# Conv and attention chain on one core: the MLP's first block ahead of the attention's last gate and residual

## The chip, the cores and the metric

The kernel runs on one core of one Trainium2 chip. The metric is the device time of one execution in microseconds; the time given is the median of three runs. The core has TensorE (matrix products, rows marked PE, and PEld for the loading of its weights), VectorE (DVE), ScalarE (ACT), GpSimd (POOL) and the sync engine (SP), each with its own list of instructions that it works off in order. What ties them together are semaphores: `wait_ge` holds an engine, and everything behind it in its list, until a count is reached, and `then_inc` raises a count when an instruction is done.

## What is computed

Four layers are applied to x of shape (4, 128, 96, 96): a mag/phase 1x1 convolution (layer 0), a selective-scan block (layer 1), a linear-attention block with an MLP (layer 2), and a 3x3 convolution with binary weights and activations (layer 3). The change lies in layer 2, between attention and MLP:

```python
ti = silu(img2tok(_dwconv(tok2img(ti), dwc_w, dwc_b)))
ta = _attn(ti, ...)                       # linear attention plus the lepe depthwise 3x3
t = shortcut + ta * act_res @ outproj_w + outproj_b
t = t + img2tok(_dwconv(tok2img(t), cpe2_w, cpe2_b))
tn2 = _ln(t, n2_g, n2_b)                  # over the 128 channels
mlp = gelu(tn2 @ fc1_w + fc1_b) @ fc2_w + fc2_b
t = t + mlp
```

## The kernel before

An image has its 128 channels on the partitions and its 96x96 pixels along them. It is cut into NB = 12 blocks of 8 rows, 768 columns. The four images are worked off one after the other, and within one image the stages follow each other. Each engine's list is made by `pipelined` or `overlapped` (L53 and L71): in round t a stage with lag l works on block t - l, and within a round the stages stand in the order in which the list names them. `overlapped` does that for several runs with a start round each. This written order is the only scheduling there is: what stands later in a list can't overtake. All counts carry a head start of 3 blocks, so waits for block b - 2 cost nothing for the first blocks.

The attention's second half, per block: TensorE computes queries, denominator, numerator and the lepe convolution; VectorE adds the lepe taps (`add_taps`, L1573, signal `f2_lepe`); GpSimd multiplies with the gate (`ta`, L711, signal `f2_ta`); TensorE projects (`project`); VectorE adds the result to the image in region 1 (`residual2`, L1590, two halves, signal `f2_t2`). GpSimd also makes the rotated queries (`turned`, L705 and L706). On GpSimd `ta` has lag 3 and `turned` lag 1; on VectorE `residual2` has lag 3 and `add_taps` lag 2.

The MLP's stage per block b:

- the cpe2 convolution of nine taps. ScalarE makes tap 0 and two terms (`first_tap` L841, `term` L862, the second of which waits for `g_t` of block b - 2), GpSimd adds the two terms (`add_term`, L678), VectorE adds taps 3 to 6 (`chain_tap`, L220), tap 7 (L1602) and tap 8 (L1607, signal `g_t`). The tiles of this chain are two per step, used in turn, and lie in region 0 over the attention's image.
- the norm. TensorE subtracts the mean with a product (`g_centre`, signal `g_yc`), ScalarE squares (`g_squares`, L957), TensorE averages (`g_variance`, into bank 6, which the projection used too), ScalarE does Ln and Exp (`g_root`, L962 and L964, with a table load ahead), VectorE multiplies (`g_normalise`, L1613, signal `g_tn`).
- the MLP. TensorE's four `up` and four `down` products, ScalarE's four Gelu (L969), VectorE's residual `x3` (L1617), ScalarE's `sign` (L974) for layer 3.

`g_centre` of block b waits for `g_tn` of block b - 1, and `up(0)` of block b for `g_tn` of block b. One round of TensorE holds ten products: four up, four down, a variance and a centre.

Before the change VectorE's list holds the whole attention and then the MLP; GpSimd's holds `ta` and `turned` of all blocks and then the additions; ScalarE waits, ahead of its MLP list, for `f2_lepe` and `f2_ta` of all twelve blocks. In round 3 of the MLP ScalarE does block 3's tap, its two terms and then block 0's root; VectorE in its round 3 does block 2's six taps and then block 0's normalise.

After the MLP's twelfth block, the next image's layer 0 (L1373 on VectorE first) follows, while layer 3 of the present one runs on TensorE (L1068).

Of the kernel before, what the change touches and what calls it, by code (L numbers as in the profile page):

```python
# [52 lines left out]
def pipelined(eng, count, stages):  # L53

    deepest = max(lag for lag, _ in stages)
    for t in range(count + deepest):
        for lag, stage in stages:
            if 0 <= t - lag < count:
                stage(t - lag, (t - lag) % 2)
# [11 lines left out]
def overlapped(eng, count, runs):  # L71

    stop = max(start + max(lag for lag, _ in stages) for start, stages in runs) + count
    for t in range(stop):
        for start, stages in runs:
            for lag, stage in stages:
                if 0 <= t - start - lag < count:
                    stage(t - start - lag, (t - start - lag) % 2)


def build(nc, t, out):

    B, _, S, _ = t["x"].shape
    NB = S // ROWS
# [12 lines left out]
    def done(i, b):  # L97

        return i * NB + (b + (1 + CREDIT))

    def steps(i, b, each, step):

        return i * (NB * each) + (b * each + step)
# [6 lines left out]
    with ctx:  # L110
# [8 lines left out]
        def pair(bank):  # L119

            return psum[:, bank:bank + 2, 0:HC]
# [9 lines left out]
        def padded(k):  # L131
            return R[k][:, 0:SP * SP].rearrange("p (h w) -> p h w", w=SP)

        def flat(k, b):
            return R[k][:, ds(BLK * b, BLK)]

        def prow(k, b, dh=0, dw=0, rows=ROWS, skip=0):

            return padded(k)[:, ds(ROWS * b + (1 + dh + skip), rows), 1 + dw:1 + dw + S]
# [3 lines left out]
        def tile(n):  # L143
            return work[:, n * BLK:(n + 1) * BLK]

        def region_tile(k, n):
            return R[k][:, n * BLK:(n + 1) * BLK]

        def halves(ap):
            return ap.rearrange("p (a c) -> p a c", a=2)  # L150
# [58 lines left out]
        def col(name, n=0, rows=slice(0, P)):  # L209
            return cols[rows, at[name] + n:at[name] + n + 1]  # L210

        def tap_weight(conv, tap):
            return col("taps", 9 * convs.index(conv) + tap_column(tap))
# [17 lines left out]
        def signal(name, owner):  # L231
            s = sem(name)
            block_signals.append((s, owner))
            return s
# [68 lines left out]
        f2_qs = signal("f2_qs", "g")  # L303
# [7 lines left out]
        f2_lepe = signal("f2_lepe", "v")  # L311
        f2_ta = signal("f2_ta", "g")
        f2_out = signal("f2_out", "p")
        f2_t2 = signal("f2_t2", "v")
# [42 lines left out]
        def all_done(eng, i, *signals):  # L357

            eng.wait_ge(ready, 1)
            for s in signals:  # L360
                k = 4 if s is g_fc1 or s is g_gelu else 1
                eng.wait_ge(s, i * (NB * k) + (NB + CREDIT) * k)
# [59 lines left out]
        def by_row(ap):  # L422
            return ap.rearrange("p (r w) -> p r w", w=S)

        def is_first(b):
            return isinstance(b, int) and b == 0
# [195 lines left out]
        def _(g):  # L622
            credit(g, "g")
            g.wait_ge(ready, 1)
            def middle(i):
# [48 lines left out]
                def add_term(conv, n):  # L674
                    def stage(b, p):
                        g.wait_ge(term_done[n], termed(i, b))
                        g.wait_ge(tap_done[n - 1], tapped(i, b))
                        g.tensor_tensor(chain_tile(conv, n, p), chain_tile(conv, n - 1, p), chain_tile(conv, n, p),  # L678
                                        ALU.add).then_inc(tap_done[n], 1)
                    return stage  # L680
# [29 lines left out]
                    g.wait_ge(f2_lepe, done(i, b))  # L710
                    g.tensor_tensor(tile(2 + p), tile(2 + p), flat(2, b), ALU.mult).then_inc(f2_ta, 1)  # L711

                pipelined(g, NB, [(3, ta), (1, turned)])

                taps = [add_term("cpe2", tap) for tap in TERM_TAPS]
                pipelined(g, NB, [(0, tap) for tap in taps])

                all_done(g, i, g_t)
                clear_frame(signs())
# [6 lines left out]
        def _(a):  # L726
# [61 lines left out]
            def middle(i, following_runs):  # L788
# [177 lines left out]
                def gelu(j):  # L966
                    def stage(b, p):
                        a.wait_ge(g_fc1, steps(i, b, 4, 4 * CREDIT + j + 1))
                        a.activation(halves(tile(4 + j)), pair(0), ACT.Gelu, bias=col("fc1_o", j)).then_inc(g_gelu, 1)  # L969
                    return stage  # L970

                def sign(b, p):
# [1 line left out]
                    a.activation(signs()[:, ds(ROWS * b + 1, ROWS), 1:1 + S],  # L974
                                 flat(3, b).rearrange("p (r w) -> p r w", w=S), ACT.Sign).then_inc(g_sign, 1)

                all_done(a, i, f2_lepe, f2_ta)
                tap, first, second = terms("cpe2", 1, 0, f2_t2, g_t)
                mlp = [(4, gelu(0)), tap, (6, sign), (4, gelu(1)), first, second, (4, gelu(2)), (3, g_root),
                       (4, gelu(3)), (2, g_squares)]  # L980
                overlapped(a, NB, [(0, mlp)] + following_runs)

# [9 lines left out]
        def _(pe):  # L992
# [7 lines left out]
            for k in range(4):  # L1000
                pe.matmul(psum[:, 1, P * (k // 2):P * (k // 2) + P], xp_r[:, P * k:P * (k + 1)], dt_r[:, P * k:P * (k + 1)],
                          start=(k % 2 == 0), stop=(k % 2 == 1))
# [24 lines left out]
            def static(ap):  # L1027
                return lambda s: ap[:, HC * s:HC * (s + 1)]
# [56 lines left out]
            def middle(i, following_runs):  # L1085
# [111 lines left out]
                turned = region_tile(3, 9)  # L1197
# [4 lines left out]
                for n in range(NT):  # L1202
                    last = pe.matmul(psum[:, 6, 300:301], region_tile(3, 10)[:, P * n:P * (n + 1)], col("one"),
                                     start=(n == 0), stop=(n == NT - 1))
# [45 lines left out]

                def g_variance(b, p):
                    pe.wait_ge(g_sq, done(i, b))
                    pe.wait_ge(g_log, done(i, b - 1))
                    product(6, [(avg128, static(tile(2 + p)))]).then_inc(g_var, 1)

# [8 lines left out]
                def down(j):  # L1264
                    def stage(b, p):
# [11 lines left out]
                mlp = [(4, up(0)), (5, down(3)), (4, up(1)), (4, down(0)), (4, up(2)), (4, down(1)),  # L1277
                       (3, g_variance), (4, up(3)), (4, down(2)), (2, g_centre)]
# [10 lines left out]
        def _(v):  # L1289
# [133 lines left out]
            def middle(i, following_runs):  # L1423
# [80 lines left out]
                left = side_tap("cpe1", 0, 0, 1, e1["centre"])  # L1504
                right = side_tap("cpe1", 0, 0, 2, e1["centre"])
# [14 lines left out]
                left = side_tap("dwc", 3, 0, 1, e2_centre)  # L1520
                right = side_tap("dwc", 3, 0, 2, e2_centre)
# [71 lines left out]

                left = side_tap("lepe", 0, 4, 1, f2_centre)
                right = side_tap("lepe", 0, 4, 2, f2_centre)
                pipelined(v, NB, [(2, left), (2, right), (0, query_phi), (1, weigh), (3, residual2), (2, add_taps)])


                def tap_7(b, p):
                    acc = by_row(chain_tile("cpe2", 2, p))  # L1600
# [3 lines left out]

                def tap_8(b, p):
                    v.wait_ge(g_tap7, done(i, b))
                    v.scalar_tensor_tensor(out=by_row(flat(3, b)), in0=prow(1, b, *TAPS[8]),  # L1607
                                           scalar=tap_weight("cpe2", TAPS[8]), in1=by_row(chain_tile("cpe2", 2, p)),
                                           op0=ALU.mult, op1=ALU.add).then_inc(g_t, 1)

                def g_normalise(b, p):
                    v.wait_ge(g_rstd, done(i, b))
                    v.tensor_tensor(halves(flat(2, b)), halves(tile(2 + p)), pair(2), ALU.mult).then_inc(g_tn, 1)  # L1613

                def x3(b, p):
# [2 lines left out]
                                           in1=halves(flat(3, b)), op0=ALU.add, op1=ALU.add).then_inc(g_x3, 1)  # L1618

                taps = [chain_tap(v, i, "cpe2", tap, 1, lambda p: chain_tile("cpe2", 2, p)) for tap in VECTOR_TAPS]  # L1620
                mlp = [(1, taps[0]), (1, taps[1]), (5, x3), (1, taps[2]), (1, taps[3]), (1, tap_7), (1, tap_8),
                       (3, g_normalise)]
                overlapped(v, NB, [(0, mlp)] + following_runs)

            overlapped(v, NB, [(0, begin(0, False)), (NB, conv_run(0))])
            for i in range(B - 1):
# [89 lines left out]
```

## Time and profile before

| | |
|---|---|
| median of 3 runs | 3650.93 us (3647.74 to 3663.47) |
| the profiled execution | 3652.96 us, span 3651.0 us |
| busy: TensorE, VectorE, ScalarE, GpSimd | 2936.3, 2437.7, 2368.8, 1101.4 us |
| TensorE's clock granted, mean of the span | 0.937 |
| data moved by DMA | 274.91 MB, mean 75 GB/s |

The row of 40 slices shows the four images as four repeats of the same pattern: TensorE at 9 tenths through most of the MLP, lower in the selective scan. A busy TensorE is not one at its peak, since the ends of pipelined products are modelled. In the timelines a row merges instructions of one line that follow each other; "x4" says how many.

### The profile page before, as it was taken

How to read it: one execution, taken by the hardware profiler on the slowest of the kernel's cores; microseconds unless marked ns; L12 is line 12 of the kernel's file. 1: busy time of each engine (PE TensorE's matmuls, PEld its weight loads, DVE VectorE, ACT ScalarE, POOL GpSimd, SP SyncE). 2: the span in 40 equal slices, each digit the busy share in tenths (PEclk: the TensorE clock that was granted, in tenths of full speed). 3: DMA queues.
4: the chain of work that ended last, by engine and by line, in shares of the span. 5: the costliest groups of instructions: out<-in, count | busy, mean ns of one | idle time of the engine just before them, and what ended most of it. 6: DMA issues, size and time to landing. Idle time of an engine off the chain costs nothing. (4 is left out here: it accounts for less than half of the span.)

```text
span 3651.0 us, 45449 instructions
## 1 busy us (share of the span) xinstructions
PE 2936.3 (80%) x17500; PEld 1593.8 (44%) x17500; DVE 2437.7 (67%) x2565; ACT 2368.8 (65%) x2681; POOL 1101.4 (30%) x612
## 2 busy tenths in 40 slices
PE   3688876969969877778996888776998788769699
PEld 2344335435534434434553433443555344354355
DVE  5787657865579657676466964768636886576761
ACT  2888545468689745437778864644868977454484
POOL 0236103642025500463103530146310453025430
PEclk9999998989999999899998999988999999989899
DMA  2001473500200157440020034643002005564101
GB/s 67 18 1 40 121 199 118 161 9 1 73 23 1 53 141 208 118 119 9 0 91 5 1 93 123 200 132 91 9 9 87 0 0 142 139 182 135 41 1 52
DMA packets 137227, 274.91 MB, mean 75 GB/s; under 512 B 17139, under 2 KB 93622, under 8 KB 137014
## 3 DMA queue, kind: packets, MB, share of 16 engines
q1 hardware_dynamic: 137014, 272.01, 26.7%
q8 instruction: 141, 2.31, 0.3%
q14 instruction: 72, 0.59, 0.1%
HBM read 194.07 MB, written 77.88 MB: 74 GB/s over the span
## 5 line engine op out<-in xcount | busy, mean ns | idle before, releaser
L1499 DVE SCALAR_TENSOR_TENSOR work<-region,cols,work 128x768 f32<-128x768 f32 x288 | 373.3, 1296 | 8.4 <-ACT work L902 3.3
L678 POOL TENSOR_TENSOR region<-region 128x768 f32<-128x768 f32 x96 | 225.4, 2352 | 350.6 <-ACT region L862 344.6
L1017 PE MATMUL psum<-region,m_fc 128*128 128x384 f32 x768 | 282.6, 491 | 11.8 <-ACT work L969 11.8
L1017 PE MATMUL psum<-region,m_cen 128*128 128x384 f32 x384 | 159.7, 541 | 158.8 <-DVE region L1613 60.9
L1270 PE MATMUL psum<-work,m_fc 128*128 128x384 f32 x768 | 282.3, 491 | 0.0
L654 POOL TENSOR_TENSOR work<-work,region 128x768 f32<-128x768 f32 x96 | 174.5, 1818 | 211.5 <-DVE work L1429 211.5
L642 POOL TENSOR_TENSOR work<-work 128x768 f32<-128x768 f32 x48 | 102.1, 2130 | 442.6 <-ACT work L783 416.1
L220 DVE SCALAR_TENSOR_TENSOR region<-region,cols 128x768 f32<-128x768 f32 x192 | 223.9, 1166 | 12.3 <-POOL region L678 8.3
L969 ACT ACTIVATE work<-psum,cols 128x768 f32<-128x768 f32 x192 | 173.1, 901 | 87.6 <-PE psum L1017 82.9
L1017 PE MATMUL psum<-work,m_avg 128*128 128x384 f32 x576 | 216.9, 500 | 16.0 <-ACT work L824 8.0
L1416 DVE SCALAR_TENSOR_TENSOR work<-region,cols,work 128x768 f32<-128x768 f32 x144 | 195.7, 1379 | 40.9 <-POOL work L642 37.5
L1017 PEld LDWEIGHTS psum<-region,m_fc 128*128 128x128 f32 x768 | 143.4, 191 | 122.8 <-ACT work L969 35.3
L693 POOL COPY region<-work 128x768 f32<-128x768 f32 x4 | 3.3, 827 | 632.9 <-DVE work L1536 632.9
L933 ACT ACTIVATE region<-psum,cols 128x768 f32<-128x768 f32 x48 | 43.2, 901 | 232.5 <-PE psum L1017 232.5
L1270 PEld LDWEIGHTS psum<-work,m_fc 128*128 128x128 f32 x768 | 142.1, 190 | 109.5 <-DVE region L1617 19.2
L1017 PEld LDWEIGHTS psum<-region,m_cen 128*128 128x128 f32 x384 | 69.4, 201 | 250.0 <-issue 117.2
L1017 PE MATMUL psum<-region,m_w_dt 128*128 128x384 f32 x384 | 147.1, 509 | 21.9 <-DVE work L1429 11.6
L1444 DVE TENSOR_TENSOR_SCAN work<-work,psum 128x768 f32<-128x768 f32 x88 | 159.6, 1814 | 3.1
L1017 PEld LDWEIGHTS psum<-work,m_avg 128*128 128x128 f32 x576 | 107.8, 193 | 108.2 <-ACT work L824 29.7
L1617 DVE SCALAR_TENSOR_TENSOR region<-psum,cols,region 128x768 f32<-128x768 f32 x48 | 48.9, 1018 | 157.5 <-PE psum L1270 157.5
L705 POOL TENSOR_TENSOR region<-work,region 128x768 f32<-128x768 f32 x48 | 90.8, 1892 | 207.8 <-DVE work L1584 207.8
L670 POOL TENSOR_TENSOR region<-work,region 64x768 f32<-64x768 f32 x48 | 115.5, 2406 | 121.0 <-DVE work L1468 121.0
(234 smaller groups left out, 7530.5 us busy)
## 6 DMA issues: line engine op xcount, KB each, us to landing
work<-scratch_cpe SPq DMA_DIRECT2D x192, 196.0 KB, 4.1
work<-scratch_dwc SPq DMA_DIRECT2D x192, 196.0 KB, 4.2
work<-scratch_lepe SPq DMA_DIRECT2D x192, 196.0 KB, 4.1
region<-in_tab_ch SPq DMA_DIRECT2D x48, 768.0 KB, 5.9
region<-in_x SPq DMA_DIRECT2D x48, 384.0 KB, 3.5
region<-in_tab_tok SPq DMA_DIRECT2D x48, 384.0 KB, 3.2
out<-work SPq DMA_DIRECT2D x48, 384.0 KB, 2.5
scratch_cpe<-region SPq DMA_DIRECT2D x44, 392.0 KB, 4.7
```

The source lines that it names most:

```text
L220: eng.scalar_tensor_tensor(out=tgt, in0=prow(k, b, *TAPS[n]), scalar=tap_weight(conv, TAPS[n]), in1=tgt, op0=ALU.mult, op1=ALU.add).then_i ...
L642: g.tensor_tensor(tile(4 + p), tile(p), tile(2 + p), ALU.add).then_inc(b_taps[0], 1)
L654: g.tensor_tensor(tile(2 + p), tile(p), flat(2, sweep_block(sweep, b)), ALU.mult).then_inc(c["du"], 1)
L670: g.tensor_tensor(flat(1, b)[0:CM], tile(2 + p)[CM:P], flat(1, b)[CM:P], ALU.mult).then_inc(d_gate, 1)
L678: g.tensor_tensor(chain_tile(conv, n, p), chain_tile(conv, n - 1, p), chain_tile(conv, n, p), ALU.add).then_inc(tap_done[n], 1)
L705: g.tensor_tensor(region_tile(3, 4 + p), tile(p), region_tile(3, 2 * p), ALU.mult).then_inc(f2_qc, 1)
L969: a.activation(halves(tile(4 + j)), pair(0), ACT.Gelu, bias=col("fc1_o", j)).then_inc(g_gelu, 1)
L1017: last = pe.matmul(psum[:, bank + s, 0:HC], weights[:, :], moving(s), start=(n == 0), stop=(n == len(terms) - 1))
L1270: last = pe.matmul(psum[:, 4 + s, 0:HC], fc2[:, P * j:P * (j + 1)], static(tile(4 + j))(s), start=(j == 0), stop=(j == 3))
L1416: v.scalar_tensor_tensor(out=by_row(tile(6 + p)) if n == 4 else sofar, in0=prow(3, b, *scan_tap(n)), scalar=col("l1taps", n), in1=sofar, o ...
L1444: v.tensor_tensor_scan(way(tile(6 + p)), way(tile(4 + p)), way(bu_flat), initial=start, op0=ALU.mult, op1=ALU.add).then_inc(c["h"], 1)
L1499: v.scalar_tensor_tensor(out=by_row(tile(acc + p)), in0=prow(k, b, *TAPS[n]), scalar=tap_weight(conv, TAPS[n]), in1=by_row(tile(acc + p)), ...
```

## The change

ScalarE's wait for all of `f2_lepe` and `f2_ta` becomes a wait for `f2_lepe` of block 6, after which the attention no longer reads the rows of region 0 on which the chain tiles lie. GpSimd's two additions of block 0 stand between `ta(10)` and `ta(11)`, those of block 1 behind `ta(11)`. On VectorE the MLP's run begins in round NB + 1 and stands ahead of the attention within a round, so block 0's six tap operations stand between `add_taps(11)` and `residual2(11)`. `g_root` of block 0 stands first in ScalarE's round 3, and `g_normalise` of block 0 first in VectorE's round 3; for all other blocks both keep their places. Two waits are added for the first block: tap 8, which writes to region 3, waits for the last `f2_qs`, since region 3 holds `turned`'s tables and results; `g_variance` waits for the last `f2_t2`, since `residual2` reads bank 6.

```diff
--- before.py
+++ after.py
@@ -710,10 +710,8 @@
                     g.wait_ge(f2_lepe, done(i, b))
                     g.tensor_tensor(tile(2 + p), tile(2 + p), flat(2, b), ALU.mult).then_inc(f2_ta, 1)
 
-                pipelined(g, NB, [(3, ta), (1, turned)])
-
                 taps = [add_term("cpe2", tap) for tap in TERM_TAPS]
-                pipelined(g, NB, [(0, tap) for tap in taps])
+                overlapped(g, NB, [(0, [(3, ta), (1, turned)]), (NB + 1, [(0, tap) for tap in taps])])
 
                 all_done(g, i, g_t)
                 clear_frame(signs())
@@ -974,9 +972,11 @@
                     a.activation(signs()[:, ds(ROWS * b + 1, ROWS), 1:1 + S],
                                  flat(3, b).rearrange("p (r w) -> p r w", w=S), ACT.Sign).then_inc(g_sign, 1)
 
-                all_done(a, i, f2_lepe, f2_ta)
                 tap, first, second = terms("cpe2", 1, 0, f2_t2, g_t)
-                mlp = [(4, gelu(0)), tap, (6, sign), (4, gelu(1)), first, second, (4, gelu(2)), (3, g_root),
+                root_first = (3, lambda b, p: g_root(b, p) if is_first(b) else None)
+                root_later = (3, lambda b, p: None if is_first(b) else g_root(b, p))
+                a.wait_ge(f2_lepe, done(i, NB // 2))
+                mlp = [root_first, (4, gelu(0)), tap, (6, sign), (4, gelu(1)), first, second, (4, gelu(2)), root_later,
                        (4, gelu(3)), (2, g_squares)]
                 overlapped(a, NB, [(0, mlp)] + following_runs)
 
@@ -1250,6 +1250,8 @@
 
                 def g_variance(b, p):
                     pe.wait_ge(g_sq, done(i, b))
+                    if is_first(b):
+                        pe.wait_ge(f2_t2, done(i, NB - 1))
                     pe.wait_ge(g_log, done(i, b - 1))
                     product(6, [(avg128, static(tile(2 + p)))]).then_inc(g_var, 1)
 
@@ -1593,8 +1595,7 @@
 
                 left = side_tap("lepe", 0, 4, 1, f2_centre)
                 right = side_tap("lepe", 0, 4, 2, f2_centre)
-                pipelined(v, NB, [(2, left), (2, right), (0, query_phi), (1, weigh), (3, residual2), (2, add_taps)])
-
+                attention = [(2, left), (2, right), (0, query_phi), (1, weigh), (3, residual2), (2, add_taps)]
 
                 def tap_7(b, p):
                     acc = by_row(chain_tile("cpe2", 2, p))
@@ -1604,6 +1605,8 @@
 
                 def tap_8(b, p):
                     v.wait_ge(g_tap7, done(i, b))
+                    if is_first(b):
+                        v.wait_ge(f2_qs, done(i, NB - 1))
                     v.scalar_tensor_tensor(out=by_row(flat(3, b)), in0=prow(1, b, *TAPS[8]),
                                            scalar=tap_weight("cpe2", TAPS[8]), in1=by_row(chain_tile("cpe2", 2, p)),
                                            op0=ALU.mult, op1=ALU.add).then_inc(g_t, 1)
@@ -1618,9 +1621,11 @@
                                            in1=halves(flat(3, b)), op0=ALU.add, op1=ALU.add).then_inc(g_x3, 1)
 
                 taps = [chain_tap(v, i, "cpe2", tap, 1, lambda p: chain_tile("cpe2", 2, p)) for tap in VECTOR_TAPS]
-                mlp = [(1, taps[0]), (1, taps[1]), (5, x3), (1, taps[2]), (1, taps[3]), (1, tap_7), (1, tap_8),
-                       (3, g_normalise)]
-                overlapped(v, NB, [(0, mlp)] + following_runs)
+                norm_first = (3, lambda b, p: g_normalise(b, p) if is_first(b) else None)
+                norm_later = (3, lambda b, p: None if is_first(b) else g_normalise(b, p))
+                mlp = [norm_first, (1, taps[0]), (1, taps[1]), (5, x3), (1, taps[2]), (1, taps[3]), (1, tap_7), (1, tap_8),
+                       norm_later]
+                overlapped(v, NB, [(NB + 1, mlp), (0, attention)] + [(NB + 1 + start, run) for start, run in following_runs])
 
             overlapped(v, NB, [(0, begin(0, False)), (NB, conv_run(0))])
             for i in range(B - 1):
```

## Rows read from the trace of the kernel before

**Rows 1.** The page, part 1: busy time of each engine.
```profile
PE 2936.3 (80%) x17500; PEld 1593.8 (44%) x17500; DVE 2437.7 (67%) x2565; ACT 2368.8 (65%) x2681; POOL 1101.4 (30%) x612
```

**Rows 2.** Table by stage: stretch, us, busy time of each engine, granted clock, DMA.
```profile
1629.00:1659.00 30.00, 5.85 (x8) 2.35 (x8) 27.74 (x21) 11.22 (x13) 16.69 (x8) 0.61 0.00 0
...
1680.00:1760.00 80.00, 77.80 (x236) 43.28 (x235) 55.68 (x48) 69.85 (x77) 29.85 (x12) 1.00 0.02 5
```

**Rows 3.** Chain that ended last, MLP of the last image: start, us, what.
```profile
3488.75 2.82 PE psum L1017 x8
3491.57 1.29 PE psum L1270 x4
...
3502.34 2.82 PE psum L1017 x8
```

**Rows 4.** Timeline of VectorE, second image: start, us, what, [idle before, releaser].
```profile
1622.78 0.95 DVE L1573 TENSOR_TENSOR work<-work,psum 128x768 f32<-128x768 f32 x1 [1.08 <-issue]
...
1628.64 1.14 DVE L1590 SCALAR_TENSOR_TENSOR region<-psum,cols,region 128x384 f32<-128x384 f32 x2 [4.90 <-PE psum L1017]
...
1631.51 8.55 DVE L220 SCALAR_TENSOR_TENSOR region<-region,cols 128x768 f32<-128x768 f32 x4 [1.73 <-POOL region L678]
...
1641.15 1.02 DVE L1607 SCALAR_TENSOR_TENSOR region<-region,cols 128x768 f32<-128x768 f32 x1
...
1648.77 2.44 DVE L1607 SCALAR_TENSOR_TENSOR region<-region,cols 128x768 f32<-128x768 f32 x1
...
1651.13 5.59 DVE L220 SCALAR_TENSOR_TENSOR region<-region,cols 128x768 f32<-128x768 f32 x4
...
1658.75 0.95 DVE L1613 TENSOR_TENSOR region<-work,psum 128x768 f32<-128x768 f32 x1
...
1659.61 4.17 DVE L220 SCALAR_TENSOR_TENSOR region<-region,cols 128x768 f32<-128x768 f32 x4
...
1674.42 0.95 DVE L1613 TENSOR_TENSOR region<-work,psum 128x768 f32<-128x768 f32 x1 [8.52 <-ACT work L964]
```

**Rows 5.** Timeline of ScalarE, the same turn.
```profile
1625.78 1.03 ACT L841 ACTIVATE region<-region,cols 128x768 f32<-128x768 f32 x1 [14.66 <-issue]
...
1645.19 0.81 ACT L957 ACTIVATE work<-psum 128x768 f32<-128x768 f32 x1 [2.05 <-PE psum L1017]
...
1653.49 0.90 ACT L962 ACTIVATE work<-psum,cols 128x768 f32<-128x768 f32 x1
...
1654.42 0.84 ACT L964 ACTIVATE work<-work 128x768 f32<-128x768 f32 x1
```

**Rows 6.** Timeline of GpSimd, the same turn.
```profile
1616.26 2.53 POOL L711 TENSOR_TENSOR work<-work,region 128x768 f32<-128x768 f32 x1
...
1623.82 1.80 POOL L711 TENSOR_TENSOR work<-work,region 128x768 f32<-128x768 f32 x1 [5.02 <-DVE work L1573]
...
1627.71 10.48 POOL L678 TENSOR_TENSOR region<-region 128x768 f32<-128x768 f32 x5 [2.09 <-ACT region L862]
```

**Rows 7.** Timeline of TensorE, the same turn.
```profile
1642.22 2.93 PE L1017 MATMUL psum<-region,m_cen 128*128 128x384 f32 x4 [13.63 <-DVE region L1607]
...
1659.84 2.90 PE L1017 MATMUL psum<-region,m_cen 128*128 128x384 f32 x4 [10.86 <-DVE region L1613]
1662.53 1.35 PE L1017 MATMUL psum<-region,m_fc 128*128 128x384 f32 x3
```

**Rows 8.** Timeline of VectorE, last image.
```profile
3408.37 0.96 DVE L1573 TENSOR_TENSOR work<-work,psum 128x768 f32<-128x768 f32 x1 [1.08 <-issue]
...
3460.46 0.95 DVE L1613 TENSOR_TENSOR region<-work,psum 128x768 f32<-128x768 f32 x1 [8.96 <-ACT work L964]
```

**Rows 9.** Table by stage, after the second image's turn.
```profile
1662.90:1676.00 13.10, 11.09 (x34) 5.95 (x33) 4.51 (x5) 11.85 (x13) 3.62 (x2) 1.00 0.08 16
```

**Rows 10.** Timeline of VectorE, from the first image's MLP into the next.
```profile
932.16 1.02 DVE L1617 SCALAR_TENSOR_TENSOR region<-psum,cols,region 128x768 f32<-128x768 f32 x1 [8.10 <-PE psum L1270]
933.09 0.55 DVE L1373 TENSOR_TENSOR region<-region 128x384 f32<-128x384 f32 x1
```

## The prediction

> **What bounds the kernel now.** The totals come first: TensorE is busy for 80% of the span, VectorE 67%, ScalarE 65%, GpSimd 30% [rows 1]. No engine is full, so the question is which wait stands last in which stage. The table by stage answers it for the place that is edited. In the MLP's steady rounds TensorE is busy 77.8 of 80 us; in the 30 us between attention and MLP of the second image it is busy 5.9 us, while VectorE is busy 27.7 [rows 2]. So TensorE sets the pace after the turn, and VectorE inside it. The chain that ended last confirms the steady part: one block enters TensorE every 13.59 us (3502.34 less 3488.75) [rows 3], and each round closes over `g_normalise`, so when the second block is normalised fixes when all later blocks are.
>
> VectorE's own sequence over the turn is then read row by row [rows 4]. `add_taps(11)` (L1573) starts at 1622.78 and ends at 1623.73. VectorE idles 4.90 us until the last projection is there, does `residual2(11)` (L1590), idles 1.73 for GpSimd, does block 0's four chain taps, tap 7 and tap 8 until 1642.17, block 1's until 1651.2, block 2's until 1658.8, and only then block 0's normalise (L1613) at 1658.75. It does block 3's taps, idles 8.52, and normalises block 1 at 1674.42. ScalarE had finished block 0's root at 1655.26 (1654.42 + 0.84) [rows 5]. ScalarE itself stood idle 14.66 us before its first cpe2 tap [rows 5], at the wait for `f2_ta`. I count each turn from the start of `add_taps(11)` to the start of the second `g_normalise`: 51.64 us here, 52.09 in the last image [rows 4, 8]; the other two images read 51.94 and 51.65.
>
> **The change, part by part** (times of the second image).
>
> (a) ScalarE no longer waits for `f2_ta`. It is free at about 1611.1, 14.66 before 1625.78 [rows 5]. Blocks 0 and 1 take three operations of about 1 us each, so both are done by 1617; the third block's wait for GpSimd's sums. Nothing in the attention stands behind them on ScalarE, so their price is zero.
>
> (b) GpSimd adds block 0's two terms between `ta(10)`, which ends at 1618.79 (1616.26 + 2.53), and `ta(11)`, which can't start before 1623.82. Two additions cost 2.10 each in the run of five (10.48 / 5) [rows 6], so they end at 1623.0 and fit in GpSimd's idle 5.02. Price zero if that cover holds; each 1 us of overrun would delay `ta(11)`, but not VectorE, which now has block 0's taps first.
>
> (c) VectorE's round: block 0's six taps stand before `residual2(11)`. They start at 1623.8 instead of 1631.51. A tap costs 1.05 alone (4.17 / 4), and 2.44 against 1.02 (the rows of L1607) when it meets a GpSimd addition, so 1.42 more for each addition met [rows 4]. Before, block 0 met three (8.55 - 4.17 = 3.1 x 1.42), block 1 two (2.44 in its last tap, 1.4 in its first four, which are shown for block 2), block 2 one (5.59 for four taps where 4.17 would do), block 3 none. Now GpSimd has `ta(11)`, block 1's two sums and the first of block 2 in block 0's stretch: four. Block 0 takes 6 x 1.05 + 4 x 1.42 = 12.0 and ends at 1635.8, 6.4 earlier. `residual2(11)` has been moved behind six taps; its two halves take 1.14 [rows 4], with a gap to 1637.1. Who waits for it: the new wait in `g_variance(0)`, and ScalarE's taps of blocks 10 and 11, more than 100 us later. Block 1 meets one sum: 6.3 + 1.4, to 1644.8.
>
> (d) The root first. TensorE's centre product starts at 1635.8; ScalarE's squares began 2.97 after it (1645.19 against 1642.22) and take 0.81; the variance product takes the same 2.97 at the low clock; Ln and Exp 0.93 + 0.84 [rows 5, 7]. That is 1635.8 + 2.97 + 0.85 + 2.97 + 1.8 = 1644.4. The table load stands in the variance's shadow. The added wait in `g_variance(0)` for `f2_t2(11)` ends at 1637.1, before the squares end at 1639.7: zero. ScalarE's block 3 taps are queued behind the root, about 3 us for nobody on the path.
>
> (e) The normalise first. Block 0 is normalised at 1644.8, when root and block 1's taps end within half a microsecond of each other: 13.9 us earlier than 1658.75.
>
> (f) What is late next. The second normalise followed the first by 15.67 us (1674.42 - 1658.75), the length of the path over TensorE and ScalarE, which would put it at 1660.5. But VectorE still owes blocks 2 and 3 before it: 0.95 for the normalise, then twice 6.3, and each block now meets two sums (block 3 met none before, because VectorE was waiting when they came): 0.95 + 2 x (6.3 + 2.84) = 19.2. The second normalise starts at 1664.0. So of 13.9 us, 3.5 are given back, and 10.4 stay. The same by idle time: 4.90 + 1.73 + 8.52 = 15.15 of VectorE's idle go, three additions more are met (9 for 6), 4.3, and 10.9 remain; the two agree within my roundings.
>
> (g) From there each round is the old one, earlier: in a steady round VectorE has idle time, TensorE none. The last block's residual hands over to the next image's first operation (L1373) in the same microsecond, and nothing else was waited for [rows 10], so an image's gain passes to the next. By image the counted turn becomes 41.3 us: gains of 10.7, 10.4, 10.4 and 10.8, **42.3 us** in sum. No DMA moves against another; SP's queue is not edited, its next loads of x shift with the MLP. Against the profiled execution (3652.96, span 3651.0) that gives 3610.7, and against the median of 3650.93, from which it stands 2 us off, **3608.6**.
>
> The uncertain price is the meeting of VectorE and GpSimd. The rows show 0 below (an addition that meets nobody) and 1.42 for each one met; nothing shows a gain. GpSimd's additions take 1.8 alone, so 1.8 is the upper end. With no additions met in block 3, the time goes to the next bound, 1660.5 or so: 13.9 an image. With 1.8 for each of nine: 3.4 less, 7.0 an image. I take 1.42, which six meetings before show without exception.
>
> By the Trainium skill ("SBUF — State Buffer", SBUF: two separate sides) the pair of ports that VectorE and GpSimd share is an exclusive lock, for two-input VectorE instructions against GpSimd reads, held for a whole instruction, so a tap can wait for a full addition. The trace agrees in kind (2.44 for 1.02). By the rule the worst sum is the 7.0 an image just worked out, by the rows 10.4.
>
> **The rivals.**
> Less contention: VectorE is not the bound at the second normalise, and the round trip of 15.67 us is. For it: ScalarE's operations could shift so that block 4's sums come after block 3's taps. Against it: my block 4 sums start at 1655.2, as block 3's taps do. 13.9 an image, 55.8 in sum: **3595**.
> More contention: seven an image, 28 in sum: **3623**. Against it: in block 0 of before, five additions in a run cost three taps 1.4 each, no more.
> Absorbed: the gain is real at the turn but a later stage of the first three images waits for something unmoved (a DMA, GpSimd's clearing). Then the last image alone counts, 10.8: **3640**. Against it: [rows 10].
> It doesn't do what it says: block 0's taps stay late, since some wait in ScalarE's or GpSimd's new order holds (the third block's first term waits for block 0's first sum). Then nothing moves: **3651**. I find no such wait for block 0.
> Slower, by TensorE's clock: the 30 us of the turn have a mean grant of 0.61 [rows 2]; its products run at 1.2 GHz and then take 2.69 (1662.53 less 1659.84) for 1.29 at 2.4 GHz [rows 3, 7]. The new order makes a second idle of about 3 us before the second normalise. If the clock stayed low over the next rounds, each round of ten products would cost 14.0 more; it decides from 0.74 of a round an image (10.4 / 14.0), and two rounds give 4 x (28 - 10.4) = 70 more: **3721**. Against it: with 10.86 us of idle before, the clock was granted in full from 1662.9, 3 us after work began again at 1659.84 [rows 7, 9].
>
> **How the numbers follow.** Forecast 0.60; less contention 0.13; more contention 0.11; absorbed 0.07; nothing 0.06; slower 0.03. The range takes the first three (0.84), with 3 to 5 us of uncertainty of the runs (before read 3647.7 to 3663.5): 3590 to 3632. One half per cent, about what a measurement can tell, is 18.3 us: faster means below 3632.7. Faster is 0.60 + 0.13 + 0.11 and 0.02 of the partly absorbed: 0.86; same 0.11; slower 0.03.
>
> **What the profile after would show.** (a) ScalarE's first cpe2 tap about 12 us before VectorE's last `add_taps`; (b) `ta(11)` at 1.0 us after `add_taps(11)` starts, as now; (c) taps directly behind it, no idle, and the residual after 13.1 us; (d, e) the first normalise 22 us after `add_taps(11)` starts, for 35.97; (f) the second after 41.3, for 51.64, with no VectorE idle between, and a pause of TensorE before it; (g) pitch 13.59 unchanged. Wrong it would be if VectorE idles before the first normalise (the root is late), if the second stays at more than 48 (contention), or if TensorE's low clock reaches beyond the second normalise.

## The result, and the profile after

The changed kernel takes 3617.82 us (median, 3604.73 to 3620.03), the kernel before 3650.68 beside it (3647.74 to 3663.47). The ratio is 0.990, with a 95% interval of 0.9883 to 0.9917: 33 us, 0.9%, faster. Forecast were 42 us. The profiled execution took 3617.15, its span is 3615.3, 35.7 less than 3651.0.

VectorE in the second image's turn after the change; it answers to [rows 4]. VectorE's line numbers are one to three higher than before: L1575 is `add_taps`, L1592 `residual2`, L1603 and L1610 taps 7 and 8, L1616 `g_normalise`, L1620 `x3`; L220 is still taps 3 to 6. On ScalarE they are two lower, so L962, which was the root's Ln, is now its Exp; L1272 on TensorE is `down`.

```profile
1614.03 0.95 DVE L1575 TENSOR_TENSOR work<-work,psum 128x768 f32<-128x768 f32 x1 [1.08 <-issue]
1614.90 8.44 DVE L220 SCALAR_TENSOR_TENSOR region<-region,cols 128x768 f32<-128x768 f32 x4
1623.37 2.44 DVE L1603 SCALAR_TENSOR_TENSOR region<-region,cols 128x768 f32<-128x768 f32 x1
1625.85 1.02 DVE L1610 SCALAR_TENSOR_TENSOR region<-region,cols 128x768 f32<-128x768 f32 x1
1626.78 1.14 DVE L1592 SCALAR_TENSOR_TENSOR region<-psum,cols,region 128x384 f32<-128x384 f32 x2
1627.84 5.59 DVE L220 SCALAR_TENSOR_TENSOR region<-region,cols 128x768 f32<-128x768 f32 x4
...
1635.45 0.95 DVE L1616 TENSOR_TENSOR region<-work,psum 128x768 f32<-128x768 f32 x1
1636.31 6.83 DVE L220 SCALAR_TENSOR_TENSOR region<-region,cols 128x768 f32<-128x768 f32 x4
...
1645.17 7.03 DVE L220 SCALAR_TENSOR_TENSOR region<-region,cols 128x768 f32<-128x768 f32 x4
...
1654.23 0.95 DVE L1616 TENSOR_TENSOR region<-work,psum 128x768 f32<-128x768 f32 x1
...
1662.10 1.02 DVE L1620 SCALAR_TENSOR_TENSOR region<-psum,cols,region 128x768 f32<-128x768 f32 x1 [4.95 <-PE psum L1272]
...
1670.45 0.95 DVE L1616 TENSOR_TENSOR region<-work,psum 128x768 f32<-128x768 f32 x1 [1.81 <-ACT work L962]
```

The three idles of [rows 4] (4.90, 1.73, 8.52) are gone: from 1614.03 to the second normalise VectorE never waits. Counted from the start of the last `add_taps`, the first three normalises of the second image come at 21.42, 40.20 and 56.42, where they came at 35.97, 51.64 and 65.23. The second is 11.4 earlier, the third only 8.8, and 8.8 it stays to the twelfth (178.8 for 187.6). What took the difference stands in TensorE's timeline of the same rounds:

```profile
1650.21 1.45 PE L1272 MATMUL psum<-work,m_fc 128*128 128x384 f32 x4
1655.32 2.90 PE L1017 MATMUL psum<-region,m_cen 128*128 128x384 f32 x4 [3.66 <-DVE region L1616]
1658.01 2.76 PE L1017 MATMUL psum<-region,m_fc 128*128 128x384 f32 x4
1660.57 1.49 PE L1272 MATMUL psum<-work,m_fc 128*128 128x384 f32 x4
...
1671.55 1.53 PE L1017 MATMUL psum<-region,m_cen 128*128 128x384 f32 x4 [0.37 <-DVE region L1616]
```

TensorE waits 3.66 us for the second normalise, and its next two products take 2.90 and 2.76 where one takes 1.53 and 1.45 at 2.4 GHz. The table by stage of the same stretch (us, busy of TensorE, weight loads, VectorE, ScalarE, GpSimd, granted clock, DMA) says why:

```profile
1653.80:1660.70 6.90, 5.38 (x9) 2.98 (x10) 3.32 (x4) 0.81 (x1) 0.00 (x0) 0.51 0.00 0
1660.70:1670.45 9.75, 9.75 (x32) 5.56 (x31) 6.43 (x6) 8.30 (x10) 4.97 (x2) 1.00 0.00 0
```

The clock was granted at 0.51 from 1653.8, still inside the pause, until 1660.7. The third normalise is 16.22 behind the second, 2.63 more than the steady 13.59 (16.43 in the last image, the same 16.2 in the others).

The sum closes. Over the four images the stretch from the last `add_taps` to the third normalise is 261.7 us before and 226.0 after: 35.7, as much as the spans differ. That it fits to a tenth is luck: the stretches between the twelfth normalise and the next image's last `add_taps` vary by 10 us among the images of before alone (704.9, 710.4 and 700.0), and only their sums agree (2115.3 before, 2115.4 after).

### The profile page after: what moved, and what is told of

Read it like the earlier page. It is cut to its first block, busy times and chain, and to the rows that moved or that the text cites. A ratio compares the mean times of both kernels' runs of the same rounds, so it can differ in the third digit from the quotient of the medians.

```text
span 3615.3 us, 45449 instructions
## 1 busy us (share of the span) xinstructions
PE 2944.2 (81%) x17500; PEld 1596.7 (44%) x17500; DVE 2452.4 (68%) x2565; ACT 2367.4 (65%) x2681; POOL 1106.2 (31%) x612
## 3 DMA queue, kind: packets, MB, share of 16 engines
q1 hardware_dynamic: 137014, 272.01, 26.9%
## 4 chain that ended last, share of the span: by engine, by line
PE 48%; DVE 27%; issue 10%; ACT 8%; DMA 4%; POOL 1%; SPq 1%; DVEq 0%; POOLq 0%; ACTq 0%
PE psum L1017 30%; PE psum L1272 5%; PE psum L1037 5%; DVE work L1418 5%; DVE work L1446 5%; PE psum L1068 3%; DVE region L220 3%; DVE region L1547 3%; DVE psum L1437 2%; DVE work L1431 2%; PE psum L1228 2%; PE psum L1229 2%; DMA work<-scratch_dwc 2%; DVE region L1491 1%; DMA region<-in_tab_tok 1%
## 5 line engine op out<-in xcount | busy, mean ns | idle before, releaser
L1272 PE MATMUL psum<-work,m_fc 128*128 128x384 f32 x768 | 282.8, 492 | 0.0
L220 DVE SCALAR_TENSOR_TENSOR region<-region,cols 128x768 f32<-128x768 f32 x192 | 239.8, 1249 | 4.0
L1272 PEld LDWEIGHTS psum<-work,m_fc 128*128 128x128 f32 x768 | 143.1, 191 | 110.8 <-DVE region L1620 19.2
L1017 PE MATMUL psum<-region,m_w_dt 128*128 128x384 f32 x384 | 147.3, 510 | 21.5 <-DVE work L1431 11.1
L1620 DVE SCALAR_TENSOR_TENSOR region<-psum,cols,region 128x768 f32<-128x768 f32 x48 | 48.9, 1018 | 168.4 <-PE psum L1272 168.4
L1037 PE MATMUL psum<-work,m_dwc_shifted 64*32 64x384 f32 x2304 | 116.5, 537 | 45.9 <-DMA work<-scratch_dwc 45.9
```

The source lines that it names most:

```text
L220: eng.scalar_tensor_tensor(out=tgt, in0=prow(k, b, *TAPS[n]), scalar=tap_weight(conv, TAPS[n]), in1=tgt, op0=ALU.mult, op1=ALU.add).then_i ...
L1017: last = pe.matmul(psum[:, bank + s, 0:HC], weights[:, :], moving(s), start=(n == 0), stop=(n == len(terms) - 1))
L1037: last = pe.matmul(psum[32 * j:32 * j + 32, bank + s, 0:HC], shifted[conv][half, c0:c0 + 32], rows[half, j, :, dw:dw + S], start=(fresh an ...
L1272: last = pe.matmul(psum[:, 4 + s, 0:HC], fc2[:, P * j:P * (j + 1)], static(tile(4 + j))(s), start=(j == 0), stop=(j == 3))
```

## The experiments

Each is an edit of the changed kernel. Turns are counted from the start of the last `add_taps`; where the images agree, one number stands for all four. "Turns" in a sum means the four stretches from there to the third normalise: 261.7 us before, 226.0 in the changed kernel. In the diffs "..." stands for lines left out.

**The pause filled.** TensorE works through its pause.

```diff
+                def fill(block, count):
+                    def stage(b, p):
+                        if isinstance(b, int) and b == block:
+                            pe.wait_ge(g_log, done(i, b - 1))
+                            for n in range(count):
+                                pe.matmul(psum[:, 6, 384:512], avg128[:, :], ident[:, :], start=True, stop=True)
+                    return stage
...
-                       (3, g_variance), (4, up(3)), (4, down(2)), (2, g_centre)]
+                       (3, g_variance), (4, up(3)), (4, down(2)), (2, fill(2, 15)), (2, g_centre)]
```

> The changed kernel, plus 15 small products (128 columns, to unused columns of bank 6) on TensorE just ahead of block 2's centre product, where TensorE pauses 3.66 us in each image before the second normalise. The products change no result. Turn times are counted from the start of the last add_taps; changed kernel: first normalise 21.42, second 40.20, third 56.43 (16.23 after the second, where a steady round is 13.59). Theory (the pause drops TensorE's clock, and the low clock lengthens the next round by 2.65): the second normalise stays at 40.2 to 40.5, the clock is not lowered after it, the third follows at 13.6 to 13.9, and four images give 9 to 11 us, a span near 3605. Rival (that round is long because VectorE or ScalarE have work left over from the turn): the second to third distance stays at 16.2 and the time at 3617.

Measured: 3604.0 us (3603.34 to 3606.23), ratio to before 0.9877 (0.9862 to 0.9892), span 3601.7. The second normalise stays at 40.2 (40.5 in the last image), the third comes 13.6 behind it, at 53.8 (54.1 in the last). TensorE's timeline, second image; L1284 is the fill, whose 15 products show as 30 rows, and L1624 the normalise:

```profile
1646.65 3.51 PE L1284 MATMUL psum<-m_ident,m_avg 128*128 128x128 f32 x30
1650.46 1.53 PE L1017 MATMUL psum<-region,m_cen 128*128 128x384 f32 x4 [0.30 <-DVE region L1624]
1651.83 1.45 PE L1017 MATMUL psum<-region,m_fc 128*128 128x384 f32 x4
```

The pause is filled for 3.51 us, the centre product waits 0.30 and takes 1.53. With the same second normalise and VectorE's list untouched, 2.6 us an image are back. So the long round was the clock's, and the clock followed the pause; work left over on VectorE or ScalarE is excluded, since it was the same here. The turns are 10.4 us shorter than the changed kernel's; the span is 13.6 shorter, the rest falling elsewhere in the images.

**The second normalise earlier.** If the pause comes from VectorE's list, the list can be mended.

```diff
+                norm_second = (3, lambda b, p: g_normalise(b, p) if b == 1 else None)
-                norm_later = (3, lambda b, p: None if is_first(b) else g_normalise(b, p))
+                norm_later = (3, lambda b, p: None if b < 2 else g_normalise(b, p))
...
-                mlp = [norm_first, (1, taps[0]), (1, taps[1]), (5, x3), (1, taps[2]), (1, taps[3]), (1, tap_7), (1, tap_8),
+                mlp = [norm_first, (1, taps[0]), (1, taps[1]), (5, x3), (1, taps[2]), (1, taps[3]), norm_second, (1, tap_7), (1, tap_8),
```

> The changed kernel, with the second block's normalise between taps 6 and 7 of block 3 on VectorE instead of behind tap 8. Theory (VectorE's list sets the second normalise, whose root is ready at 36.9; the pause sets the clock): the second normalise comes at 37.2 to 37.6 for 40.20, TensorE's pause shrinks from 3.66 to under 1 us, the clock stays high and the third follows at 13.6, at 51 for 56.43: 5.4 an image, 21 us in all, a time near 3596. Rival (the debt of VectorE is only moved: two taps of block 3, six of block 4 and a residual still stand before the third normalise): the third normalise comes at 54 or later, 9 us in all or less, a time of 3608 or more.

Measured: 3592.76 us (3589.5 to 3593.58), ratio to before 0.9846 (0.9829 to 0.9863). The second normalise comes at 38.1 to 38.5, the third at 51.7 to 52.1 in three images and at 53.4 in the first, where a stretch of 3.4 us at the low clock, from 40.2 on, remained. TensorE's wait for it, second image, and VectorE's next rounds:

```profile
1647.61 1.53 PE L1017 MATMUL psum<-region,m_cen 128*128 128x384 f32 x4 [1.29 <-DVE region L1616]
```
```profile
1646.52 0.95 DVE L1616 TENSOR_TENSOR region<-work,psum 128x768 f32<-128x768 f32 x1
...
1651.76 1.02 DVE L1620 SCALAR_TENSOR_TENSOR region<-psum,cols,region 128x768 f32<-128x768 f32 x1 [0.33 <-PE psum L1272]
...
1660.10 0.95 DVE L1616 TENSOR_TENSOR region<-work,psum 128x768 f32<-128x768 f32 x1 [1.81 <-ACT work L962]
```

VectorE's debt (two taps of block 3, a residual, six taps of block 4) fits in the round with 1.81 to spare, so the rival falls. The second normalise is about 0.8 later than I expected, since the four taps ahead of it met GpSimd twice and ended behind the root (7.15 us in the second image, for 4.17; they ended at 38.6, the root at 37.6). This version beats both kernels. Its turns are 16.7 us shorter than the changed kernel's (226.0 - 209.3): 1.7 to 2.1 an image by the earlier normalise, 2.6 to 2.9 in three images and 1.0 in the first by the clock. The median is 25 us lower than the changed kernel's; the 8 us beyond the turns lie in stretches whose lists are the same, so the time came out near the expected 3596 partly by luck.

**The same with a short fill** (six products ahead of the centre product, the fill of above).

> The kernel with the second block's normalise between taps 6 and 7, plus 6 small products on TensorE ahead of block 2's centre product (unused columns of bank 6, no result changed). Without the products one image of four still had a granted clock of 0.50 from 40.2 to 43.6, and its third normalise came 15.3 after the second for 13.6 in the others. Theory (that is the same mechanism, by the pause of 1.3 us and its position): all four images have 13.6 and the low stretch after the second normalise is gone; 0 to 2 us less than without the products, a time of 3588 to 3593, so within the measurement. Rival (six products only delay the centre product): the third normalise comes 1 us later in every image, 4 us more in all.

Measured: 3593.04 us (3588.86 to 3596.12), ratio 0.9868 (0.9849 to 0.9886), not distinguishable from the one without, whose interval overlaps. The kernel before took 3641.89 us beside this run and the two single runs of `fill_turn` and `small_adds` below, where it took 3650.43 beside the others, so times of the two groups can't be compared directly; the turns can. In its profile all four images have 13.6 between second and third normalise, and no low stretch follows the second; the turns sum to 207.2, for 209.3 without the fill. The clock part is as expected; the time lies at the upper edge of what I had given and tells nothing. In one execution each this can't prove that the short fill always helps: three of four images were without a low stretch before it.

**The turn alone**: `g_root` and `g_normalise` of block 0 at their old places.

```diff
-                mlp = [root_first, (4, gelu(0)), tap, (6, sign), (4, gelu(1)), first, second, (4, gelu(2)), root_later,
+                mlp = [(4, gelu(0)), tap, (6, sign), (4, gelu(1)), first, second, (4, gelu(2)), (3, g_root),
...
-                mlp = [norm_first, (1, taps[0]), (1, taps[1]), (5, x3), (1, taps[2]), (1, taps[3]), (1, tap_7), (1, tap_8),
-                       norm_later]
+                mlp = [(1, taps[0]), (1, taps[1]), (5, x3), (1, taps[2]), (1, taps[3]), (1, tap_7), (1, tap_8),
+                       (3, g_normalise)]
```

> The changed kernel with g_root and g_normalise of block 0 at their old places, so only the turn (block 0's taps ahead of the last gate and residual, ScalarE's early start) is left. By my steps: first normalise at about 30.6 (root late behind block 3's terms, normalise behind block 2's taps), second 15.7 later at 46.3, set by the path over TensorE and ScalarE and not by VectorE, third 13.6 later at 59.9: 5.3 an image against before, 21 in all. If the turn alone brought all, the third normalise would come at 56.4.

Measured: normalises at 30.46, 46.1 to 46.5 and 59.7 to 60.1; time 3625.22 in one run. VectorE, second image:

```profile
1647.46 0.94 DVE L1616 TENSOR_TENSOR region<-work,psum 128x768 f32<-128x768 f32 x1
1648.32 4.17 DVE L220 SCALAR_TENSOR_TENSOR region<-region,cols 128x768 f32<-128x768 f32 x4
...
1663.54 0.95 DVE L1616 TENSOR_TENSOR region<-work,psum 128x768 f32<-128x768 f32 x1 [8.93 <-ACT work L962]
```

VectorE again waits 8.93 for the second root: without the early normalise the path over TensorE and ScalarE is the bound, as before. The turn alone is worth 22.0 us over the four images (261.7 - 239.7).

**The order alone**: the lists of before at the turn, with root and norm first.

```diff
-                overlapped(g, NB, [(0, [(3, ta), (1, turned)]), (NB + 1, [(0, tap) for tap in taps])])
+                pipelined(g, NB, [(3, ta), (1, turned)])
+                pipelined(g, NB, [(0, tap) for tap in taps])
...
-                a.wait_ge(f2_lepe, done(i, NB // 2))
+                all_done(a, i, f2_lepe, f2_ta)
...
-                overlapped(v, NB, [(NB + 1, mlp), (0, attention)] + [(NB + 1 + start, run) for start, run in following_runs])
+                pipelined(v, NB, attention)
+                overlapped(v, NB, [(0, mlp)] + following_runs)
```

> The kernel before with g_root and g_normalise of block 0 first in their rounds, without the turn. By my steps: first normalise at 28.4 for 35.97, but VectorE then owes blocks 2 and 3, so the second comes at 47.2 for 51.63 with a pause of TensorE of about 3 us before it, the clock drops, and the third is at 63.4 for 65.23: 1.8 an image, 7 in all. If VectorE's debt did not count, the second would come 15.7 after the first, at 44.1, and the gain would be 7.5 an image, 30 in all.

Measured: 26.9, 46.0 and 61.1 to 61.2 in three images (28.0, 47.1 and 63.5 in the first); 3638.66 us in one run, 14.9 us over the turns (261.7 - 246.8), twice what I expected. VectorE, second image (lines one higher again):

```profile
1647.29 0.95 DVE L1617 TENSOR_TENSOR region<-work,psum 128x768 f32<-128x768 f32 x1
...
1666.40 0.94 DVE L1617 TENSOR_TENSOR region<-work,psum 128x768 f32<-128x768 f32 x1
```

The mechanism is as expected: the second normalise is 19.1 behind the first and VectorE never waits between them. The sizes were off twice. Block 1's taps met one GpSimd addition where I had kept two (block 3's terms stand behind the root now), 1.4 us. And after the pause the clock cost 2.8 us in one image and 1.4 to 1.6 in three, where the low stretch was 3.4 us long for 6.9. (In the first image the first normalise waited 1.03 for its root, behind a variance product of 2.93 at the low clock.) The two halves give 22.0 and 14.9 and together 35.7: nearly additive, 1.2 less.

**TensorE kept busy in the turn**, ahead of the first centre product, where it idles after the last projection.

```diff
+                def warm(block, count):
+                    def stage(b, p):
+                        if isinstance(b, int) and b == block:
+                            pe.wait_ge(f2_phiz, done(i, NB - 1))
+                            for n in range(count):
+                                pe.matmul(psum[:, 2, 384:512], avg128[:, :], ident[:, :], start=True, stop=True)
+                    return stage
...
-                       (3, g_variance), (4, up(3)), (4, down(2)), (2, g_centre)]
+                       (3, g_variance), (4, up(3)), (4, down(2)), (2, warm(0, 24)), (2, g_centre)]
```

> The changed kernel, plus 24 small products (128 columns, to unused columns of bank 2) on TensorE ahead of block 0's centre product, in the idle after the last projection. The products change no result. Theory (before the second normalise VectorE's list is the bound and TensorE's clock costs nothing): centre and variance of block 0 run faster than 2.97 us, the root is ready earlier, but the first normalise stays at 21.42, the second at 40.2 and the third at 56.4. Rival (the low clock at the turn costs time too): the first normalise moves 1 to 2 us earlier, and the second with it.

Measured: first normalise at 21.45 in three images and 23.1 in the last, second at 39.7 (40.6 in the last), third at 56.2 in two images, 54.7 in the first and 55.9 in the last; 3608.26 in one run. TensorE, second image (48 rows are the 24 products):

```profile
1618.18 6.92 PE L1284 MATMUL psum<-m_ident,m_avg 128*128 128x128 f32 x48
1624.93 1.46 PE L1017 MATMUL psum<-region,m_cen 128*128 128x384 f32 x4
```

The centre product takes 1.46 where it took 2.93, and in three images the first normalise doesn't move: the low clock ahead of it costs nothing there, because VectorE's list is the bound. The last image shows what an earlier root can do instead:

```profile
3394.09 2.66 DVE L1618 SCALAR_TENSOR_TENSOR region<-region,cols 128x768 f32<-128x768 f32 x1
```
```profile
3394.14 1.80 POOL L678 TENSOR_TENSOR region<-region 128x768 f32<-128x768 f32 x1 [4.06 <-ACT region L860]
```

The root is ready 1.3 earlier than in the changed kernel (18.7 for 20.1), so ScalarE's terms of block 3 behind it are earlier too, and GpSimd's addition of them begins 1.3 earlier (20.6 for 21.9). In the last image it begins 0.05 us behind the start of block 1's tap 8 (L1618), which takes 2.66 for 1.02; in the others it begins 0.08 to 0.23 behind it, and the tap keeps its 1.02. There block 2's first four taps take 6.29 for 6.83, which is the 0.5 by which the second normalise comes earlier; neither theory had it. The run's time lies 9 us under the changed kernel's median, but its turns account for 2.9 of them (226.0 - 223.1), and the kernel before was itself 8.8 lower beside this run (3641.89 for 3650.68).

**The meetings removed.** GpSimd's additions for blocks 0 to 4 are cut to 64 of 768 columns, so that VectorE has almost nothing to wait for. In the other 704 columns of these blocks a part of the convolution's terms is left out, so this kernel computes something else there.

```diff
+                        cut = slice(0, 64) if isinstance(b, int) and b < 5 else slice(0, BLK)
-                        g.tensor_tensor(chain_tile(conv, n, p), chain_tile(conv, n - 1, p), chain_tile(conv, n, p),
-                                        ALU.add).then_inc(tap_done[n], 1)
+                        g.tensor_tensor(chain_tile(conv, n, p)[:, cut], chain_tile(conv, n - 1, p)[:, cut],
+                                        chain_tile(conv, n, p)[:, cut], ALU.add).then_inc(tap_done[n], 1)
```

> The changed kernel with GpSimd's cpe2 additions cut from 768 to 64 columns for blocks 0 to 4 of each image, so the terms of the other columns are left out of the result there. Only VectorE's meetings with these additions go; the gate of block 11 still meets a tap. Theory (each meeting costs VectorE 1.42 on the path): block 0's taps end 4.3 earlier, the first normalise is at 17.2, then set by the root, and the second at 32.9, set by the path over TensorE and ScalarE (15.7 after the first), the third at 46.5, without TensorE's long pause: 10 an image, 40 us in all, near 3578. Rival (the taps are slow for another reason, such as ScalarE's terms running beside them): the first normalise stays within 1 us of 21.4 and the second near 40.

Measured: in the first and third image 17.23, 32.4 to 32.9 and 46.0 to 46.5; in the second and fourth 15.86, 30.2 and 43.8; 3573.33 us in one run. The turns sum to 180.0, 46.0 less than in the changed kernel, where I expected 40. VectorE, third image (L1617 is the normalise, L963 the root's Exp):

```profile
2481.01 5.59 DVE L220 SCALAR_TENSOR_TENSOR region<-region,cols 128x768 f32<-128x768 f32 x4
...
2489.68 4.17 DVE L220 SCALAR_TENSOR_TENSOR region<-region,cols 128x768 f32<-128x768 f32 x4
...
2497.36 0.95 DVE L1617 TENSOR_TENSOR region<-work,psum 128x768 f32<-128x768 f32 x1 [1.40 <-ACT work L963]
...
2512.51 0.95 DVE L1617 TENSOR_TENSOR region<-work,psum 128x768 f32<-128x768 f32 x1 [1.80 <-ACT work L963]
```

Block 0's four taps take 5.59 for 8.44 (the gate's multiplication still meets one), block 1's 4.17 for 5.59, and tap 7 of block 0 takes 1.02 for 2.44; no instruction of VectorE or ScalarE was changed. So the taps are slow by these meetings, 1.42 each. Both normalises now wait for their root, and as soon as they do, TensorE's clock is on the path: in the second and fourth image it was granted in full from 12.2 on, in the first and third low until 21.5 and 15.9, and the first normalise differs by 1.37.

## Why the prediction was right, and where it was off

The direction, the time (3617.8 within 3590 to 3632) and the mechanism up to the second normalise were right; the gain was 9 us smaller than forecast, because the round behind the second normalise was not the old one.

(a), (b) held. ScalarE's first cpe2 tap starts at 1602.29, right behind its last attention work, 11.7 ahead of the last `add_taps`. GpSimd's first two additions took 4.51 from 1610.01, for 4.2 expected, and `ta(11)` started at 1615.06, 1.03 after `add_taps(11)` began, as before. (c) The residual started 12.75 after `add_taps`, expected 13.1. (d) and (e) The first normalise came at 21.42, expected 22.0, with the root 1.3 ahead of it (ScalarE's Exp ended at 1634.11). The root was earlier than worked out, since the variance product took 1.56 and not 2.97: the clock was granted in full between 15.9 and 22.7. The wait added to `g_variance` cost nothing: the product started at 1630.75, 0.06 behind the end of the squares.

(f) held as to mechanism, and this was the step that carried most: the gain at the first normalise, 14.5, isn't kept; VectorE then owes two blocks, and the second normalise comes 18.8 behind the first, at 40.2 for 41.3 expected. Four meetings were counted in block 0's stretch, one in block 1's and two in each of the next two, and the sums of the rows agree (8.44 and 2.44; 5.59; 6.83; 7.03). I was 1.1 us too high because each stretch was taken 0.1 to 0.4 too long: operations were added up at their full time, while the next one starts up to 0.1 before the end, and the two meetings of block 2 cost 2.66 for 2.84. The turn alone showed the other bound (8.93 of waiting for the second root), the small additions the price of a meeting.

(g) failed. "From there each round is the old one" left out the clock: the third normalise came 16.2 behind the second for 13.59, 10.8 us over four images, and with the pause filled it came 13.6 behind again in all four. I had named the pause and the low clock, as the slower rival, and then set its price in the forecast to zero, because after 10.86 us of idle before, the clock was back 3 us into the work. That row was read wrongly: those 3 us were slow there too (a product of 2.90 instead of 1.53), but they lay in the turn, ahead of a second normalise that had to wait for them anyway, so the old 51.64 already held their cost. A new pause brings a new one. The size is half of the low stretch's products, not a whole round: 2.63 an image, from the gain of 11.4 to 8.8. The slower rival's own condition, a low clock over most of a round, didn't occur; the stretch was 6.9 us, half a round. But one of the signs of being wrong that the prediction itself named, a low clock reaching beyond the second normalise, did: it reached 6.5 us beyond (46.7 for 40.2).

The four turns sum to a gain of 35.7, where the forecast had 42.3: 4.2 more by the second normalise (207.3 before, 160.8 after, 46.5), 10.8 less by the round behind it. The two errors partly cancel, which is luck. The median differs by 33: the executions of the changed kernel lie between 3604.7 and 3620.0. The stretch from the twelfth normalise to the next image's last `add_taps` varies between 700.0 and 710.4 us in the profile of before alone and is not touched by the change. Why it varies was not tested.

The rivals: less contention didn't happen (nine meetings, as counted), nor more; absorbed is excluded by the time, since the last image's gain alone (9.0) is far from 33, and the stretches behind the turns are no longer in sum than before; that nothing moves, by the three idles gone. The lock of the Trainium skill ("SBUF — State Buffer", SBUF: two separate sides), held for a whole instruction, agrees with the small additions in kind: with 64 columns for 768 block 1's taps took 4.17 for 5.59. Its worst case, a whole addition of 1.8 for each meeting, wasn't reached: in a run of alternating operations each cost 1.42, and the dearest single one, in the last image of `fill_turn`, 1.64 (2.66 for 1.02).

## What to carry to other kernels

When an operation is moved forward in an engine's list, find the next one of its kind: what the engine now owes before it (here two blocks of taps, 19 us) takes the place of the path that bound it, and part of the gain goes back. Moving the second one forward inside that debt, here behind ten of the twelve taps, gave 1.7 to 2.1 us an image and shortened TensorE's pause besides. And ask of a new pause of TensorE what the products behind it would cost at half clock, even where it is short; where the list can't be mended, fifteen small products into unused columns of PSUM bought 2.6 us an image.

## What the runs showed of the hardware that I had not expected

A pause of 3.7 to 4.0 us on TensorE came with 6.9 us of 0.5 clock in all four images; with the second normalise earlier the pause was 1.3 in two images and 1.7 in the third, without a low stretch, and 1.9 in the first, with one of 3.4 us that began 1.0 after it. The low stretch of 6.9 us begins inside the pause, 1.5 us before its end (39.8 against 41.3), so that most of it falls on the work after it. The length of the pause alone doesn't give the cost: with the order alone pauses of 5.2 us in three images had a low stretch of only 3.4 us, which cost 1.4 to 1.6, where 3.7 us of pause in the changed kernel cost 2.6. What decides between the two wasn't tested. And the clock costs nothing where another engine is the bound: with TensorE kept busy ahead of the first centre product this product took 1.46 for 2.93, and in three of four images the first normalise stayed where it was; in the fourth the earlier root shifted a GpSimd addition onto a tap, and it came 1.6 later.
